# Routed rows of a mixture-of-experts layer: 31 pair tiles and nine single tiles in place of 39 pair tiles

## The chip, the cores and the metric

The kernel runs on one core of one Trainium2 chip. The metric is device time in microseconds (us) of one execution. Before the change the median of three executions is 734.16 us (734.12 to 734.52). What differs by less than about 0.2% (1.5 us) can hardly be told from no change.

## The reference

4096 tokens of 128 numbers pass through a feed-forward block, an attention-like block and the same feed-forward block again. The kernel's two feed-forward layers are the part that matters here:

```
x = x + 0.5 * ffn(layernorm(x))
# ffn(flat), E = 8 experts, TOPK = 2, F = 512, D = 128
probs = softmax(flat @ gate_W.T);  top_v, top_i = top_k(probs, 2)
g = silu(flat @ w1_e[e]);  u = flat @ w3_e[e];  out_e = (g * u) @ w2_e[e]
routed = sum over the two chosen experts of gate * out_e
shared = (silu(flat @ w1_s) * (flat @ w3_s)) @ w2_s / 8
ffn = 0.5 * shared + 0.5 * routed
```

Each token is multiplied with the weights of its two chosen experts only. So 8192 rows (token, expert) are sorted by expert and computed in tiles of 128 rows; each expert's rows are padded to whole units.

## The kernel before, in words

The program is written out by engine (`block.tensor`, `block.vector`, `block.scalar`, `block.gpsimd`, `block.sync`), with semaphores by hand. `pipelined(eng, stages, count, ...)` writes out steps k = 0, 1, 2, ...; in step k each stage works on item k minus its lag, in the order in which the stages are listed.

A feed-forward layer l (0 or 1) has these parts.

* **Norm, scores, shared part.** TensorE transposes the normalised tokens and computes gate scores. The shared weights need no routing, so `in_shared` (six matmuls of 512 columns) and `out_shared` (into `psH`) start before the routing is known and fill TensorE while VectorE, ScalarE and TensorE make the routing tables.
* **Routing.** VectorE picks two experts for each token, TensorE ranks the rows (`rank`), and `slots_of` (L826 to L856) turns ranks into row positions: a chain of small VectorE instructions, each waiting for the one before it (`route.then`). Two `shared_steps(1)` around it hand one shared tile each to TensorE. Then 16 batches: VectorE's `batch` (L866, L869), ScalarE's `pairs` (L1165, L1168) and TensorE's `batch` (L1421, columns 2 x `TILES_R`) invert the permutation; `table` (L889 to L902) gives `source` and `target`, and `experts` gives `w_off`, the expert of each pair.
* **Routed part.** GpSimd fetches the rows of each tile with an indirect DMA (`fetch_row`, L626) and later scatters the results (`send_result`, L641); the fetch of group g (four tiles) stands with the send of group g - 5. TensorE, step by step: `in_routed` (lag 4), `look_up` (lag 5: the register reads of the expert offset), `out_routed` (lag 6), and the transposes of the next group's rows (`transpose_rows`, L1433, four at once in every fourth step). Layer 0 leaves one chunk of the shared part (four shared tiles) for after the routed part, layer 1 two chunks; layer 0 goes on to the attention, layer 1 loads `YF` (both results of each token) and adds them.

A pair is 256 rows of one expert. ScalarE copies the pair's weights in two parts of an fp32 split (`weights_of`, L1229: `w_high`, `w_low`, 128 x 1024 each). In `in_routed` 128 x 128 pieces of these weights are stationary and the 256 rows move, so the hidden values come out with the hidden index on the partitions, as `out_routed` needs them as its stationary side:

```
for j in range(FT // PT):
    f = s.u % PT * (FT // PT) + j
    i = product(out[:, s.u % 2, j * PAIR:(j + 1) * PAIR], w_high[n][:, w, cols],
                w_low[n][:, w, cols], high, low)
```

For each tile that makes twelve matmuls of 256 columns (six for `psG`, six for `psU`); ScalarE applies silu (L1155), VectorE multiplies (`gated_routed`, L954, into `hT`), and `out_routed` (L1487) does four fp32 matmuls, which appear as eight instructions. `copy_y` (L980, the last group: `copy_y_last`, L966) scales four tiles' results by their gates into `yout`.

With 39 pairs there are RUN = 78 tiles in GROUPS = 20 groups, the last with LAST = 2 tiles.

## Time and profile before

| | |
|---|---|
| median of three executions | 734.16 us (734.12 to 734.52) |
| span of the profiled execution | 733.5 us; its own device time is not listed, the three executions lie 0.6 to 1.0 us above this span |
| TensorE matmul busy | 660.3 us, 90% of the span |
| TensorE weight load busy | 602.1 us, 82% |
| VectorE, ScalarE, GpSimd busy | 458.8, 411.3, 430.6 us |
| routed part, layer 0 / layer 1 | 112.4 to 301.8 us / 512.3 to 701.5 us |
| attention | about 316 to 440 us |

Matmuls are pipelined: an instruction's own duration is longer than the distance from its start to the next one's start, so the distance between starts, not the mean duration, tells what a matmul costs in a stream. "Busy" counts the union of overlapping instructions. A row's bracket gives the time that the engine sat idle before it and the instruction that ended the wait.

### The profile page before, as it was taken

To read this page: it belongs to the slowest core of one execution; us is meant where nothing else is said; L and a number is where in the kernel's file an instruction comes from. 1 tells how busy PE (TensorE), PEld (TensorE's weight loads), DVE (VectorE), ACT (ScalarE), POOL (GpSimd) and SP (SyncE) were. 2 spreads that over 40 slices of the span, in tenths; PEclk is the share of its full clock that TensorE was granted. 3 is DMA by queue.
4 is the path that set the end of the run, shared out by engine and by line. 5 is a ranking of instruction groups with operands and counts; after the bars stand their busy time and mean duration, and the time that the engine had idled before them with its cause. 6 is when DMAs were issued, how large, how long until landed. Compare 5 with 4: busy or idle time off the path is not lost.

```text
span 733.5 us, 14294 instructions
## 1 busy us (share of the span) xinstructions
PE 660.3 (90%) x4860; PEld 602.1 (82%) x4860; DVE 458.8 (63%) x1177; ACT 411.3 (56%) x861; POOL 430.6 (59%) x511
## 2 busy tenths in 40 slices
PE   3878999999999999957987777999999999999995
PEld 3767879999999999825654574888999999999983
DVE  6678895554445555359999867884555555544536
ACT  2658617666666666236654436664666666666520
POOL 5600075777777776489987424007577777777530
PEclk9989999999999999989999997999999999999999
DMA  9542011221222231131100002402212212212137
GB/s 296 231 78 40 1 42 38 56 52 52 52 55 52 52 53 44 57 105 44 47 12 1 0 1 46 73 2 49 40 55 54 52 52 56 51 53 52 43 104 261
DMA packets 35685, 45.91 MB, mean 63 GB/s; under 512 B 6432, under 2 KB 27936, under 8 KB 35232
## 3 DMA queue, kind: packets, MB, share of 16 engines
q1 hardware_dynamic: 25632, 24.39, 11.8%
q0 software_dynamic: 9984, 20.63, 11.5%
q8 instruction: 40, 0.66, 0.4%
q14 instruction: 29, 0.24, 0.1%
HBM read 28.41 MB, written 16.58 MB: 61 GB/s over the span
## 4 chain that ended last, share of the span: by engine, by line
PE 65%; DVE 20%; issue 4%; ACT 4%; POOL 3%; DMA 2%; SPq 1%; ACTq 0%; POOLq 0%; DVEq 0%
PE psY L1487 18%; PE psG L1334 6%; PE psU L1336 6%; PE psG L1336 6%; PE psU L1335 6%; PE psG L1335 6%; PE psU L1334 6%; PE psH L1405 4%; DVE rec L1076 3%; PE psT L1433 2%; DVE hs L748 2%; DVE XN L738 2%; DVE ln_stats L725 1%; DVE xn L1060 1%; POOL results L641 1%
## 5 line engine op out<-in xcount | busy, mean ns | idle before, releaser
L626 POOL DMA_INDIRECT rows<-tokens,source x156 | 153.7, 985 | 156.3 <-DVE source L900 98.6
L1155 ACT ACTIVATE silu<-psG 128x512 f32<-128x512 f32 x220 | 131.1, 596 | 150.6 <-PE psG L1336 147.2
L954 DVE TENSOR_TENSOR hT<-silu,psU 128x512 f32<-128x512 f32 x156 | 107.4, 688 | 158.9 <-PE psU L1336 150.3
L641 POOL DMA_INDIRECT results<-yout,target x156 | 153.8, 986 | 63.3 <-issue 45.7
L1487 PE MATMUL psY<-W,hT 128*128 x1232 | 162.4, 275 | 1.8 <-DVE yout L980 1.8
L1487 PEld LDWEIGHTS psY<-W,hT 128*128 128x128 f32 x1232 | 150.4, 191 | 2.2 <-DVE hT L954 2.2
L1229 ACT ACTIVATE w_high<-W13H 128x1024 fp32r x78 | 82.7, 1061 | 59.0 <-PE psU L1336 54.8
L1334 PE MATMUL psG<-xTH,w_high 128*128 128x256 f32 x312 | 100.0, 321 | 0.7 <-ACT w_low L1229 0.7
L1336 PE MATMUL psG<-xTH,w_low 128*128 128x256 f32 x312 | 88.0, 282 | 0.0
L1336 PE MATMUL psU<-xTH,w_low 128*128 128x256 f32 x312 | 88.0, 282 | 0.0
L1335 PE MATMUL psU<-xTL,w_high 128*128 128x256 f32 x312 | 87.7, 281 | 0.0
L1335 PE MATMUL psG<-xTL,w_high 128*128 128x256 f32 x312 | 87.4, 280 | 0.0
L1334 PE MATMUL psU<-xTH,w_high 128*128 128x256 f32 x312 | 86.9, 278 | 0.0
L1229 ACT ACTIVATE w_low<-W13L 128x1024 fp32r x78 | 81.8, 1048 | 0.0
L748 DVE TENSOR_TENSOR hs<-silu,psU 128x512 f32<-128x512 f32 x64 | 43.7, 684 | 38.3 <-PE psU L1336 30.5
L1405 PEld LDWEIGHTS psH<-W2S,hs 128*128 128x128 f32 x512 | 59.4, 192 | 5.7 <-DVE hs L748 4.7
L1405 PE MATMUL psH<-W2S,hs 128*128 128x128 f32 x512 | 60.1, 276 | 2.9 <-DVE hs L748 2.9
L1334 PEld LDWEIGHTS psG<-xTH,w_high 128*128 128x128 f32 x312 | 59.2, 190 | 0.9 <-issue 0.9
L1335 PEld LDWEIGHTS psG<-xTL,w_high 128*128 128x128 f32 x312 | 59.3, 190 | 0.0
L1334 PEld LDWEIGHTS psU<-xTH,w_high 128*128 128x128 f32 x312 | 59.1, 190 | 0.0
L1336 PEld LDWEIGHTS psG<-xTH,w_low 128*128 128x128 f32 x312 | 58.8, 188 | 0.0
L1335 PEld LDWEIGHTS psU<-xTL,w_high 128*128 128x128 f32 x312 | 58.6, 188 | 0.0
(188 smaller groups left out, 1215.7 us busy)
## 6 DMA issues: line engine op xcount, KB each, us to landing
W<-w_e SPq DMA_DIRECT2D x3, 2048.0 KB, 13.7
tokens<-XN SPq DMA_DIRECT2D x16, 260.0 KB, 5.9
Y<-results SPq DMA_DIRECT2D x32, 128.0 KB, 2.2
YF<-results SPq DMA_DIRECT2D x16, 256.0 KB, 5.9
rows<-tokens,source POOLq DMA_INDIRECT x156
results<-yout,target POOLq DMA_INDIRECT x156, 2.3
X<-x SPq DMA_DIRECT2D x8, 256.0 KB, 5.5
out<-X SPq DMA_DIRECT2D x8, 256.0 KB, 2.8
```

What stands on the lines that cost most here:

```text
L626: pool.indirect_dma_start(rows[:, slot(l, g), t, :], None, tokens, bass.IndirectOffsetOnAxis(ap=source[:, tile:tile + 1], axis=0))\
L641: pool.indirect_dma_start(results, bass.IndirectOffsetOnAxis(ap=target[:, tile:tile + 1], axis=0), yout[:, g % 2, t, :], None).then_inc(y_ ...
L748: dve.tensor_tensor(hidden, silu[:, s.u % 2, :], psU[:, s.u % 2, :], ALU.mult).then_inc(h_done, 1)
L954: dve.tensor_tensor(hT[:, s.u // PT % 2, half, :].rearrange("p f c -> p (f c)"), silu[:, s.u % 2, :], psU[:, s.u % 2, :], ALU.mult).then_i ...
L1076: dve.reciprocal(rec[:, s.u, :, :], den[:, s.u, :, :]).then_inc(y_link, 1)
L1155: act.activation(silu[:, s.u % 2, :], psG[:, s.u % 2, :], ACT.Silu).then_inc(silu_done, 1)
L1229: act.activation(used[p % 2][:, :, :], kept[:, :, bass.ds(entries[p], F)], ACT.Copy)\
L1334: pe.matmul(out, a_high, b_high, start=True, stop=False)
L1335: pe.matmul(out, a_high, b_low, start=False, stop=False)
L1336: return pe.matmul(out, a_low, b_high, start=False, stop=True)
L1405: i = pe.matmul(psH[:, par, t * D:(t + 1) * D], hs[:, par, f, t * P:(t + 1) * P], W2S[:, f, :], start=(f == 0), stop=(f == FT - 1))
L1487: i = pe.matmul(into[:, t * D:(t + 1) * D], hT[:, s.u // PT % 2, f, s.u % PT * P:(s.u % PT + 1) * P], W2[:, bass.ds(at + f * D, D)], start ...
```

## The change

There are PAIRS = 31 pairs, followed by SINGLES = 9 single tiles of 128 rows: UNITS = 40, RUN = 71 tiles, 18 groups, the last with three tiles. An expert with n tiles gets n // 2 pairs and, for an odd n, one single (with more than 31 pairs in all, those beyond become singles). A single tile is computed the other way round: its rows (`xTH`, `xTL`, 128 x 128) are stationary and the expert's weights move, 512 columns each, straight out of `W13H` and `W13L`: six matmuls of 512 columns and no copy by ScalarE. The hidden values then come out with the rows on the partitions, so VectorE writes them into `hrow`, TensorE turns them with four transposes into `psH` (`turn_hidden`), ScalarE copies `psH` into `turned` (`copy_turned_h`), and `out_routed` takes `turned`. `slots_of` gets more instructions, and `TILES_R` falls from 78 to 71.

```diff
-PAIRS = TOPK * NT // PAIR + E - 1
-RUN = PT * PAIRS
+PAIRS = 31
+SINGLES = 9
+UNITS = PAIRS + SINGLES
+RUN = PT * PAIRS + SINGLES
...
-        last_y = [psY, psT]
+        last_y = [psY, psT, psH[:, 0, :]]
...
+                    route.then(dve.tensor_tensor_scan(single_at[:, 1:E + 1], ones[:, 0:E], nsingle[:, :], 0.0,
+                                                      ALU.mult, ALU.add))
...
+                    route.then(dve.tensor_tensor(beyond, cum[:, :, :], wide(singles_from[:, :], ET_FLAT), ALU.is_gt))
+                    route.then(dve.tensor_tensor(beyond, beyond, wide(moved_by[:, :], ET_FLAT), ALU.mult))
+                    route.then(dve.tensor_tensor(cum[:, :, :], cum[:, :, :], beyond, ALU.add))
...
+                    if s.i >= PT * PAIRS:
+                        dve.tensor_tensor(hrow[:, s.i % 2, :], silu[:, s.u % 2, :], psU[:, s.u % 2, :], ALU.mult)\
+                           .then_inc(h_done, 1)
+                        return
...
+                def copy_turned_h(i):
+
+                    act.wait_ge(turned_psum, SINGLES * l + i - PT * PAIRS + 1)
+                    act.activation(turned[:, i % 2, :, :].rearrange("p f c -> p (f c)"), psH[:, i % 2, :], ACT.Copy)\
+                       .then_inc(turned_done, 1)
...
+                    if k - 1 >= PT * PAIRS:
+                        copy_turned_h(k - 1)
...
+                    if s.i >= PT * PAIRS:
+                        at = table_entry(l, s)
+                        own_high, own_low = xTH[:, par, s.u % GT, :], xTL[:, par, s.u % GT, :]
+                        for out, w, used, full in ((psG, 0, silu_done, g_full), (psU, 1, h_done, u_full)):
+                            pe.wait_ge(used, turn - 1)
+                            product(out[:, s.u % 2, :], own_high, own_low, W13H[:, w, bass.ds(at, F)],
+                                    W13L[:, w, bass.ds(at, F)]).then_inc(full, 1)
+                        return
...
+                def turn_hidden(s):
+
+                    if s.i < PT * PAIRS:
+                        return
+                    pe.wait_ge(h_done, s.i + first_routed[l] + 1)
+                    for f in range(FT):
+                        i = pe.transpose(psH[:, s.i % 2, f * P:(f + 1) * P], hrow[:, s.i % 2, f * P:(f + 1) * P],
+                                         ident[:, :])
+                    i.then_inc(turned_psum, 1)
...
+                pipelined(pe, [(in_routed, 4), (turn_hidden, 5), (look_up_in, 3), (look_up, 5), (out_routed, 6),
+                               (transpose_later, 0)], RUN, 2 * GT, straight=True)
```

The order of instructions shows the two places on which most rests. First TensorE in the routed part. Before, the second half of a pair's `in_routed` and the `out_routed` behind it (TENSOR_LOAD and ISA are register reads; twelve matmuls of 256 columns make one tile, the first four stand above this piece):

```order
L1335 MATMUL psG<-xTL,w_high 128x256
L1336 MATMUL psG<-xTH,w_low 128x256
L1334 MATMUL psU<-xTH,w_high 128x256
L1335 MATMUL psU<-xTL,w_high 128x256
L1336 MATMUL psU<-xTH,w_low 128x256
L1334 MATMUL psU<-xTH,w_high 128x256
L1335 MATMUL psU<-xTL,w_high 128x256
L1336 MATMUL psU<-xTH,w_low 128x256
L1345 TENSOR_LOAD w_off
L1345 ISA x2
L1494 ISA x2
L1487 MATMUL psY<-W,hT 128x128 x4
```

Of the changed kernel, a step among the single tiles:

```order
L1385 MATMUL psU<-W13H,xTH 128x512
L1386 MATMUL psU<-W13L,xTH 128x512
L1387 MATMUL psU<-W13H,xTL 128x512
L1544 MATMUL psH<-ident,hrow 128x128 x4
L1397 TENSOR_LOAD w_off
L1397 ISA x2
L1575 ISA
L1576 ISA
L1569 ISA
L1562 MATMUL psY<-W,turned 128x128 x4
L1385 MATMUL psG<-W13H,xTH 128x512
```

The `psU` matmuls belong to tile i + 1, the transposes to tile i, and the `psY` matmuls to tile i - 1: the four transposes and one more register read per tile stand between them.

Second VectorE in `slots_of`, between the ranks and the first batch. Before:

```order
L830 TENSOR_SCALAR pair_bits<-psY 128x8
L831 TENSOR_SCALAR pair_bits<-pair_bits 128x8
L833 CAST npair<-pair_bits 128x8
L834 SCALAR_TENSOR_TENSOR tend<-ones,npair 128x8
L836 TENSOR_TENSOR tstart<-tend,npair 128x8
L837 SCALAR_TENSOR_TENSOR base<-tstart,psY 128x8
```

In the changed kernel, from behind `base` on (up to `base` there is one instruction more than before):

```order
L858 TENSOR_TENSOR nsingle<-pair_at 128x8
L860 SCALAR_TENSOR_TENSOR nsingle<-nsingle,ntile 128x8
L862 SCALAR_TENSOR_TENSOR single_at<-ones,nsingle 128x8
L865 TENSOR_SCALAR singles_from<-pair_at 128x8
L866 SCALAR_TENSOR_TENSOR moved_by<-pair_at,single_at 128x8
L868 TENSOR_SCALAR moved_by<-moved_by 128x8
L870 SCALAR_TENSOR_TENSOR chosen<-base,chosen 128x8
L872 SCALAR_TENSOR_TENSOR cum<-not_first,chosen 128x256
L764 TENSOR_TENSOR hs<-silu,psU 128x512
L879 TENSOR_TENSOR pick<-cum,singles_from 128x256
L880 TENSOR_TENSOR pick<-pick,moved_by 128x256
L881 TENSOR_TENSOR cum<-cum,pick 128x256
```

In all, seven small instructions more than before stand ahead of the scan and the shared tile (`hs`), and three of 128 x 256 behind it.

## Rows read from the trace of the kernel before

**Rows 1.** The page, part 1: TensorE's busy time, share of the span and instructions
```profile
PE 660.3 (90%) x4860; PEld 602.1 (82%) x4860; DVE 458.8 (63%) x1177; ACT 411.3 (56%) x861; POOL 430.6 (59%) x511
```

**Rows 2.** Windows: busy time of each engine by stretch, then granted clock, DMA share, GB/s
```profile
55.00:70.00 15.00, 13.08 (x95) 10.98 (x95) 14.15 (x54) 13.20 (x44) 0.00 (x0) 1.00 0.34 49
...
150.00:200.00 50.00, 50.00 (x437) 50.00 (x436) 25.02 (x46) 32.84 (x43) 38.25 (x39) 1.00 0.21 53
...
450.00:470.00 20.00, 18.80 (x96) 14.06 (x95) 19.25 (x66) 10.10 (x37) 0.24 (x1) 0.79 0.64 107
```

**Rows 3.** Timeline of TensorE, routed part: start us, length us, instruction
```profile
119.74 1.05 PE L1487 MATMUL psY<-W,hT 128*128 x8
...
122.05 1.05 PE L1487 MATMUL psY<-W,hT 128*128 x8
122.94 0.60 PE L1433 MATMUL psT<-ident,rows 128*128 128x128 f32 x4
...
124.79 1.05 PE L1487 MATMUL psY<-W,hT 128*128 x8
```

**Rows 4.** Timeline of TensorE, shared part: matmuls of 512 columns
```profile
61.28 0.39 PE L1335 MATMUL psU<-XNTL,W13SH 128*128 128x512 f32 x1
...
61.52 0.39 PE L1336 MATMUL psU<-XNTH,W13SL 128*128 128x512 f32 x1
```

**Rows 5.** Timeline, first matmul of the routed part, layer 0
```profile
112.42 0.36 PE L1334 MATMUL psG<-xTH,w_high 128*128 128x256 f32 x1 [0.70 <-ACT w_low L1229]
```

**Rows 6.** Timeline, all engines, end of the routed part of layer 0
```profile
299.24 0.69 DVE L980 TENSOR_TENSOR yout<-psY,gate 128x512 f32<-128x512 f32 x1
...
300.07 1.13 PE L1487 MATMUL psY<-W,hT 128*128 x8 [0.87 <-DVE yout L980]
...
300.20 0.97 POOL L641 DMA_INDIRECT results<-yout,target  x1 [4.43 <-DVE yout L980]
...
301.85 0.48 PE L1334 MATMUL psG<-XNTH,W13SH 128*128 128x512 f32 x1
...
306.59 0.97 POOL L641 DMA_INDIRECT results<-yout,target  x1 [0.30 <-issue]
```

**Rows 7.** The same for layer 1 and what follows it
```profile
701.50 0.48 PE L1334 MATMUL psG<-XNTH,W13SH 128*128 128x512 f32 x1
...
706.22 0.97 POOL L641 DMA_INDIRECT results<-yout,target  x1 [0.30 <-issue]
...
715.59 0.69 DVE L1001 TENSOR_TENSOR X<-X,YF 128x512 f32<-128x512 f32 x1 [6.13 <-DMA YF<-results]
...
716.93 0.50 PE L1334 MATMUL psU<-XNTH,W13SH 128*128 128x512 f32 x1 [1.28 <-DVE hs L748]
```

**Rows 8.** Timeline, routing of layer 0: slots_of on VectorE, and who waits behind it
```profile
50.90 0.17 DVE L831 TENSOR_SCALAR pair_bits<-pair_bits 128x8 int32<-128x8 int32 x1
...
51.10 0.17 DVE L833 CAST npair<-pair_bits 128x8 f32<-128x8 int32 x1
...
57.63 0.56 ACT L1165 ACTIVATE pair<-in_tile,partition 128x312 bf16<-128x312 bf16 x1 [1.80 <-DVE in_tile L866]
...
62.54 0.43 PE L1421 MATMUL psT<-pair,at_place 128*128 128x156 bf16 x4 [0.64 <-ACT pair L1168]
```

**Rows 9.** The same wait of TensorE in layer 1
```profile
468.50 0.43 PE L1421 MATMUL psT<-pair,at_place 128*128 128x156 bf16 x4 [0.64 <-ACT pair L1168]
```

**Rows 10.** Groups, shapes kept apart: busy us, mean ns of one, idle us before
```profile
L847 DVE TENSOR_TENSOR pick<-cum,onehot 128x256 f32<-128x256 f32 x4 | 2.5, 617 | 0.1
...
L796 DVE TENSOR_TENSOR onehot<-rev_e,row_b 128x256 f32<-128x256 f32 x4 | 1.7, 424 | 0.1
...
L1168 ACT ACTIVATE pair<-in_tile 128x78 bf16<-128x78 bf16 x128 | 23.2, 253 | 0.0
L1165 ACT ACTIVATE pair<-in_tile,partition 128x312 bf16<-128x312 bf16 x32 | 17.5, 548 | 5.5 <-DVE in_tile L866 5.5
...
L1133 ACT ACTIVATE XNT<-psH 128x512 f32<-128x512 f32 x10 | 6.0, 595 | 10.7 <-PE psH L1380 10.5
```

More of the change, by code:

```diff
@@ L275, in macaron @@
         cum = memory["cum"]
-        pair_cmp = memory["pair_cmp"]
+        unit_cmp = memory["unit_cmp"]
         memory = overlaid(
             [("hT", [P, 2, FT, PAIR], fp32),
-             ("yout", [P, 2, GT, D], fp32)],
+             ("yout", [P, 2, GT, D], fp32),
+             ("hrow", [P, 2, F], fp32)],
             [("XN", [P, TILES, ROW], fp32)])
@@ L284, in macaron @@
         yout = memory["yout"]
+        hrow = memory["hrow"]
         XN = memory["XN"]
@@ L325, in macaron @@
              ("w_high1", [P, 2, F], fp32r)],
+            [("below_turned", [P, 6 * 2 * F], fp32),
+             ("turned", [P, 2, FT, P], fp32)],
             [("XNTL", [P, NT], fp32r), ("XNTH", [P, NT], fp32r)])
@@ L344, in macaron @@
         w_low = [memory[f"w_low{n}"] for n in range(2)]
+        turned = memory["turned"]
         psG = ps("psG", [P, 2, 512])
@@ L405, in macaron @@
         y_psum = sem("y_psum")
+        turned_psum = sem("turned_psum")
+        turned_done = sem("turned_done")
         y_done = sem("y_done")
@@ L829, in slots_of @@
                     dve.wait_ge(ranked, l + 1)
-                    route.then(dve.tensor_scalar(pair_bits[:, 0, :], psY[:, E:2 * E], float(PAIR - 1), None, ALU.add))
-                    route.then(dve.tensor_scalar(pair_bits[:, 1, :], pair_bits[:, 0, :], PAIR.bit_length() - 1, None,
+                    route.then(dve.tensor_scalar(tile_bits[:, 0, :], psY[:, E:2 * E], float(P - 1), None, ALU.add))
+                    dve.tensor_scalar(tile_bits[:, 1, :], tile_bits[:, 0, :], P.bit_length() - 1, None,
+                                      ALU.logical_shift_right)
@@ L835, in slots_of @@
                                                       ALU.mult, ALU.add))
-                    route.then(dve.tensor_tensor(tstart[:, :], tend[:, :], npair[:, :], ALU.subtract))
-                    dve.scalar_tensor_tensor(base[:, :], tstart[:, :], float(PAIR), psY[:, 0:E], ALU.mult, ALU.add)\
+                    route.then(dve.tensor_scalar(pair_at[:, 1:E + 1], pair_sum[:, :], float(PAIRS), None, ALU.min))
+                    dve.scalar_tensor_tensor(base[:, :], pair_at[:, 0:E], float(PAIR), psY[:, 0:E], ALU.mult, ALU.add)\
@@ L873, in experts @@
                 def experts():
[L875 to L879 removed]
+                    for first, n, at in ((0, PAIRS, pair_at), (PAIRS, SINGLES, single_at)):
+                        cmp3 = [P, n, E]
+                        i = dve.tensor_tensor(unit_cmp[:, first:first + n, :], wide(unit_no[:, 0:n], cmp3),
+                                              at[:, 1:E + 1].unsqueeze(1).to_broadcast(cmp3), ALU.is_ge)
+                    route.then(i)
+                    route.then(dve.tensor_reduce(unit_e[:, :], unit_cmp[:, :, :], X_AXIS, ALU.add))
+                    dve.tensor_scalar(w_off[:, :], unit_e[:, :], float(E - 1), float(F),
                                       ALU.min, ALU.mult).then_inc(w_off_done, 1)
@@ L1484, in out_routed @@
                     t = s.u % GT
-                    into = last_y[t % 2] if s.i >= RUN - LAST else psY
+                    into = last_y[t] if s.i >= RUN - LAST else psY
                     for f in range(FT):
-                        i = pe.matmul(into[:, t * D:(t + 1) * D], hT[:, s.u // PT % 2, f, s.u % PT * P:(s.u % PT + 1) * P],
+                        hidden = turned[:, s.i % 2, f, :] if single else \
+                            hT[:, s.u // PT % 2, f, s.u % PT * P:(s.u % PT + 1) * P]
+                        i = pe.matmul(into[:, t * D:(t + 1) * D], hidden,
                                       W2[:, bass.ds(at + f * D, D)], start=(f == 0), stop=(f == FT - 1))
@@ L1491, in look_up, with look_up_in @@
                 def look_up(s):
-                    if s.u % PT == 0:
+                    if s.u % PT == 0 or s.i >= PT * PAIRS:
                         for f in range(FT):
                             pe.lower_ap(W2[:, bass.ds(table_entry(l, s) + f * D, D)])
-                pipelined(pe, [(in_routed, 4), (look_up, 5), (out_routed, 6), (transpose_later, 0)], RUN, 2 * GT,
-                          straight=True)
+                def look_up_in(s):
+                    if s.i >= PT * PAIRS:
+                        at = table_entry(l, s)
+                        for w in range(2):
+                            pe.lower_ap(W13H[:, w, bass.ds(at, F)])
+                            pe.lower_ap(W13L[:, w, bass.ds(at, F)])
+                pipelined(pe, [(in_routed, 4), (turn_hidden, 5), (look_up_in, 3), (look_up, 5), (out_routed, 6),
+                               (transpose_later, 0)], RUN, 2 * GT, straight=True)
                 def sum_results(n):
```

59 lines of the change are left out of this document (38 added, 21 removed).

## The prediction

 Each of the two routed parts takes 189 us: layer 0 from 112.42 [rows 5] to 301.85, where the first shared matmul behind it starts [rows 6]. Together they are half of the span. There a tile less is a tile's TensorE time less, and a TensorE instruction more is paid in full. In the routing stretches it is otherwise: between 55 and 70 us VectorE is busy 14.15 of 15 us, between 450 and 470 us 19.25 of 20 [rows 2], and TensorE waits 0.64 us at a time for ScalarE's `pair`, which itself waited for VectorE's `in_tile` [rows 8, 9].
>
> **Prices on TensorE.** The starts count, not the durations. From one `psY` block to the next are 122.05 - 119.74 = 2.31 us: one tile's `in_routed` and `out_routed`. The eight `psY` instructions take 122.94 - 122.05 = 0.89 us of it, so twelve matmuls of 256 columns take 1.42 us, 0.118 each. With the four row transposes a step takes 124.79 - 122.05 = 2.74 us, so four transposes cost 0.43 to 0.44 us, 0.11 each [rows 3]. A matmul of 512 columns costs 61.52 - 61.28 = 0.23 to 0.24 us [rows 4]; six of them are 1.38 us over the stretch that I read. Check: 78 x 2.31 + 19 x 0.44 + the wait of 0.87 us [rows 6] = 189.4 us, as measured.
>
> **What each routed part loses.** Seven tiles less (78 to 71): 7 x 2.31 = 16.2 us, and their row transposes, 7 x 0.11 = 0.8 us. The wait of 0.87 us for `yout` at the end [rows 6] goes as well: it arises because the first tile of the last group comes right behind the last tile of the group before, with no `in_routed` between; with a last group of three tiles an `in_routed` and four transposes lie there (1.82 us), more than VectorE's 0.69 us. Sum 17.8 us.
>
> **What it gains.** Nine singles: 9 x 0.44 = 4.0 us for turning the hidden values. Their `in_routed` costs 6 x 0.23 = 1.38 against 1.42 us, 9 x 0.04 = 0.4 us less. ScalarE's new copy of 128 x 512 costs 0.60 us like the copy of the same form [rows 10], while two weight copies per pair fall away; I cost it at nothing on TensorE, because between the transposes of tile i and `out_routed` of tile i lie `out_routed` of tile i - 1 (0.89) and the next step's `in_routed` and transposes (1.82): 2.7 us of cover for some 0.8 us. Likewise between the end of `in_routed` i and its transposes lie 0.44 + 0.89 + 1.38 = 2.7 us, for VectorE's 0.69 us. Without that cover it would cost what the rivals say. Only for the very last tile, with no `in_routed` behind it, do I add 0.1 us. Sum 3.7 us; TensorE's routed part gets 14.1 us shorter.
>
> **Where it reaches the result.** What follows the routed part waits for GpSimd's last send, which starts 306.59 - 301.85 = 4.74 us after TensorE is through: six sends of 1.28 us, (306.59 - 300.20) / 5 apart, queued behind the last full group [rows 6]. Now there are seven, but TensorE still has 1.38 + 2 x 0.44 + 3 x 0.89 + 0.1 = 5.0 us to go after the last full group; it had 301.85 - 299.2 = 2.65. So the last send starts at 1.0 (yout and start) + 6 x 1.28 - 5.0 = 3.7 us after TensorE's end, 1.1 us sooner. In layer 0 that is 14.1 + 1.1 = 15.2 us. In layer 1, VectorE stands 6.13 us waiting for `YF`, and TensorE at 716.93 waits 1.28 us for VectorE in turn [rows 7]; the loads decide, and TensorE's lag of 1.1 us is within its slack: 15.2 us again. Together 30.4 us.
>
> **GpSimd** issues 142 DMAs a layer in place of 156: 14 x 1.28 = 17.9 us less, more than TensorE loses, so it is no nearer to being the bound. The removed weight copies on ScalarE (16 in a layer) were hidden and bring nothing.
>
> **What the routing costs.** `slots_of` has seven more small instructions at 51.10 - 50.90 = 0.20 us each [rows 8], 1.4 us, and three of 128 x 256. The nearest forms take 0.42 (L796) and 0.62 us (L847) [rows 10], with 0.04 us between two; they read and write in order like the first, so I take 0.46 each, 1.4 us; the upper bound is 2.0. VectorE is the bound there and hands over to ScalarE and by it to TensorE [rows 2, 8, 9], so 2.8 us arrive. Back come: ScalarE's smaller `pair` copies, (548 - 253) / (312 - 78) = 1.26 ns an element [rows 10], 56 elements a batch, 0.07 us for each of some six batches that are bound by it, 0.4 us; and 64 `psT` matmuls of 142 in place of 156 columns, at 0.23 us for 512 [rows 4] 0.4 us. Net 2.0 us a layer, 4.0 in all. It has bounds of 0 (slack of VectorE takes it up before TensorE notices) and 3.4 a layer (nothing given back).
>
> **Sum.** 30.4 - 4.0 = 26.4 us off the span of 733.5 us: 707.1. The three executions lie 0.6 to 1.0 above that span; from their median of 734.16 I forecast **707.8 us**. The unknown terms alone (routing 0 to 6.8, the cover of the last tile, 0.23 or 0.24 for a matmul) give 704 to 711.
>
> **A rule that speaks against it.** The row shows four transposes in 0.60 us, starting 0.11 apart, so the fourth alone lasts 0.27 [rows 3]. The Trainium skill's page "TensorE: Matmul & The Clock Gate", section "Part 4: PE-mode transpose", gives about 275 ns for a transpose of 128 x 128 in one kernel, and most of it as access latency. Read as a cost of each, it would make 72 transposes dearer by 0.165 us each, 11.9 us, and the sum 719.7; the duration agrees with the trace, the spacing says that it overlaps. The same section says that transposes do not count as busy for the clock. Both are rivals below, worked out from rows.
>
> **Rivals.**
> * **Routing hidden.** VectorE's 2.8 us are taken up by its waits. For it: it waits 1 to 2 us in some places of the shared part. Against it: TensorE is nearly full behind 70 us and can't catch up what it has lost. 707.8 - 4.0 = 703.8.
> * **A handoff shows.** Three engines in turn (VectorE's `hrow`, TensorE, ScalarE's `turned`) per single where there was one. If the copy and its start, 0.6 + 0.2 us, stand in TensorE's way in each of 18 tiles, 14.4 us: 722.2; in part, or by the register reads now made for every single, 712 to 716. Against it: the cover of 2.7 us above.
> * **Transposes don't overlap.** 4 x 0.27 = 1.08 in place of 0.44 us, 18 times: 11.5 us, 719.3. Against it: [rows 3].
> * **Serial singles, slower than before.** The place is the step of a single: if one `psH` or `hrow` half or the order made each tile wait for the whole chain of the same tile, it would take 1.38 + 0.85 (product and start) + 0.60 (transposes to their end) + 0.8 + 0.89 = 4.5 us in place of 2.7: 18 x 1.8 = 32.4 us, 740.2. It turns the sign from 1.46 us a tile on (26.4 / 18). For it: nothing in the order, which puts tile i + 1 and i - 1 around tile i.
> * **Clock, slower than before.** If the stretch of singles, with 0.44 of 2.7 us in transposes, were granted 1.2 GHz, 18 x 2.7 = 48.8 us come on top: 756.6. Against it: the routed part is granted 1.00 with a group of transposes in every fourth step [rows 2, 3].
> * **Nothing gained.** Another queue sets the end and the time stays near 734. No row speaks for it.
>
> **How the numbers follow.** Forecast 0.62; routing hidden 0.15; a handoff shows 0.14; transposes don't overlap 0.03; serial 0.03; clock 0.02; nothing 0.01. Faster by more than 0.2% (1.5 us, about what can be told from no change): 0.62 + 0.15 + 0.14 + 0.03 = 0.94; within 0.01; slower 0.05. The range of 703 to 718 takes in the forecast's own 704 to 711, the hidden routing and the lower half of the handoffs; it leaves out 0.07 + 0.03 + 0.03 + 0.02 + 0.01 = 0.16.
>
> **What would show it.** Right: among the singles, `psY` blocks about 2.7 us apart and no idle time before `psH` or `psY`; the first routed matmul about 2 us later in layer 0 and 2 us more in its distance from the routing of layer 1; TensorE's routed part 175 us long; the last send 3.7 us behind it. Wrong: idle time before `psY` released by ScalarE's `turned` or before `psH` released by VectorE's `hrow`; transposes 0.27 us apart; a granted clock under 1.00 at the end of the routed part; or a routed part that starts as early as before, which would move the time towards 703.8.

## The result and the profile after

The changed kernel took 712.42 us (median of four executions, 711.56 to 713.63) against 734.34 us (734.12 to 735.35, four executions) of the kernel before on the same chip: a ratio of 0.9701, 95% interval 0.9688 to 0.9714. It is 21.9 us faster, where 26.4 were forecast. The sign was right and the time lies in the stated range of 703 to 718; it is 4.6 us above the forecast's 707.8, and also above the 704 to 711 that the prediction's own unknown terms gave. One execution of the second experiment below took 1337.39 us and is outside its ratio.

The page of the changed kernel, part 1, answers to [rows 1]:

```profile
PE 637.3 (90%) x4530; PEld 573.0 (81%) x4530; DVE 443.3 (62%) x1167; ACT 382.3 (54%) x833; POOL 402.0 (57%) x485
```

TensorE has 330 matmuls and 23.0 us of busy time less, and is still busy for 90% of the span. What bounds the kernel is the same engine as before. Windows at the same places of the program as in [rows 2] (the third starts 9.4 us behind the `row_a` of layer 1, as there):

```profile
55.00:70.00 15.00, 11.93 (x79) 9.39 (x79) 14.06 (x50) 11.25 (x34) 0.00 (x0) 1.00 0.29 48
...
150.00:200.00 50.00, 50.00 (x433) 50.00 (x432) 24.68 (x45) 31.89 (x41) 38.11 (x40) 1.00 0.21 54
...
438.41:458.41 20.00, 18.66 (x86) 13.96 (x84) 19.00 (x69) 7.81 (x28) 0.23 (x1) 0.70 0.60 109
```

In the routing (first window) TensorE does less in the same time, 79 instructions in place of 95, since VectorE, busy for 14.06 of 15 us, hands over later. In the third window the granted clock is 0.70, where it was 0.79. That isn't what moves the routing: in the experiment with both operands at 32 the same stretch has

```profile
436.92:456.92 20.00, 15.31 (x86) 11.05 (x84) 19.00 (x69) 7.70 (x28) 0.21 (x1) 0.93 0.57 109
```

with VectorE busy for the same 19.00 us, and from `row_a` to the first routed matmul it takes 73.71 us, against 73.84. In the routed part TensorE is full as before, but the second window has 433 instructions in place of 437. That small row turns out to be most of the error.

**The singles.** Timeline of TensorE in layer 0, where the singles begin (start us, length us, instruction):

```profile
268.09 0.60 PE L1544 MATMUL psH<-ident,hrow 128*128 128x128 f32 x4
268.53 1.06 PE L1562 MATMUL psY<-W,hT 128*128 x8
270.83 0.60 PE L1544 MATMUL psH<-ident,hrow 128*128 128x128 f32 x4
271.27 1.06 PE L1562 MATMUL psY<-W,turned 128*128 x8
272.16 0.49 PE L1485 MATMUL psT<-ident,rows 128*128 128x128 f32 x3
273.89 0.60 PE L1544 MATMUL psH<-ident,hrow 128*128 128x128 f32 x4
```

From `psH` to `psH` are 270.83 - 268.09 = 2.74 us, the forecast's "about 2.7"; four transposes delay the `psY` block behind them by 271.27 - 270.83 = 0.44 us, and no row shows idle time before `psH` or `psY`. The chain VectorE, TensorE, ScalarE is covered. A single's own turn, all engines:

```profile
276.62 0.60 PE L1544 MATMUL psH<-ident,hrow 128*128 128x128 f32 x4
276.89 0.69 DVE L992 TENSOR_TENSOR hrow<-silu,psU 128x512 f32<-128x512 f32 x1 [0.78 <-PE psU L1387]
...
277.26 0.60 ACT L1283 ACTIVATE turned<-psH 128x512 f32<-128x512 f32 x1 [0.54 <-PE psH L1544]
...
279.79 1.06 PE L1562 MATMUL psY<-W,turned 128*128 x8
```

`turned` is ready at 277.86 and needed at 279.79, where the `psY` block of that tile starts: 1.9 us to spare. ScalarE waits 0.54 us for the transposes; nobody waits for that wait. The groups say the same for all 18 singles:

```profile
L1283 ACT ACTIVATE turned<-psH 128x512 f32<-128x512 f32 x18 | 10.7, 597 | 10.1 <-PE psH L1544 10.1
...
L1544 PE MATMUL psH<-ident,hrow 128*128 128x128 f32 x72 | 10.8, 272 | 0.0
```

The 10.1 us of idle time are ScalarE's, which is busy for 54% of the span; TensorE's idle time before `psH` is 0.0.

**Start and end of the routed parts**, which answer to [rows 5, 6, 7]:

```profile
114.55 0.36 PE L1385 MATMUL psG<-xTH,w_high 128*128 128x256 f32 x1 [0.72 <-ACT w_low L1271]
...
287.32 0.96 POOL L657 DMA_INDIRECT results<-yout,target  x1 [6.14 <-DVE yout L1022]
...
288.88 0.60 PE L1544 MATMUL psH<-ident,hrow 128*128 128x128 f32 x4
...
290.21 1.12 PE L1562 MATMUL psH<-W,turned 128*128 x8
...
291.08 0.47 PE L1385 MATMUL psG<-XNTH,W13SH 128*128 128x512 f32 x1
...
294.96 0.97 POOL L657 DMA_INDIRECT results<-yout,target  x1 [0.30 <-issue]
...
679.20 0.47 PE L1385 MATMUL psG<-XNTH,W13SH 128*128 128x512 f32 x1
...
683.09 0.97 POOL L657 DMA_INDIRECT results<-yout,target  x1 [0.30 <-issue]
```

The routed part of layer 0 is 291.08 - 114.55 = 176.53 us long (189.43 before), the last `psY` block (its output is `psH` there) has no wait for `yout` before it, and the last send starts 3.88 us behind TensorE's end (4.74 before).

**Where the 23.7 us went**, from the starts of the same instructions in both traces:

| stretch | before | after | difference | forecast |
|---|---|---|---|---|
| start to first routed matmul, layer 0 | 112.42 | 114.55 | +2.13 | +2.0 |
| routed part, layer 0 | 189.43 | 176.53 | -12.90 | -14.1 |
| to the last send | 4.74 | 3.88 | -0.86 | -1.1 |
| last send to `row_a` of layer 1 | 134.00 | 134.04 | +0.04 | 0 |
| `row_a` to the first fetch of layer 1 | 53.65 | 55.56 | +1.91 | +2.0 |
| first fetch to first routed matmul | 18.06 | 18.28 | +0.22 | 0 |
| routed part, layer 1 | 189.20 | 176.36 | -12.84 | -14.1 |
| to the last send | 4.72 | 3.89 | -0.83 | -1.1 |
| last send to the end | 27.28 | 26.71 | -0.57 | 0 |
| span | 733.5 | 709.8 | -23.7 | -26.4 |

The first and the last row hold a part that isn't the change's. The same program profiled again has its first routed matmul at 113.70, 0.85 us sooner, and ends 27.49 us behind the last send, 0.78 us later; all rows between repeat to 0.04 us. Where the 0.85 us come from shows at VectorE's first `row_a`, ahead of everything that the change touches (the kernel before, the changed kernel, and the changed kernel again):

```profile
36.10 0.41 DVE L800 TENSOR_REDUCE row_a<-logit 128x32 f32<-128x256 f32 x1
```

```profile
36.30 0.41 DVE L816 TENSOR_REDUCE row_a<-logit 128x32 f32<-128x256 f32 x1
```

```profile
35.49 0.41 DVE L816 TENSOR_REDUCE row_a<-logit 128x32 f32<-128x256 f32 x1
```

From there to the first routed matmul are 76.32, 78.25 and 78.21 us: the routing of layer 0 costs 1.93 and 1.89 us, beside 1.91 in layer 1. So the routing's two terms came as forecast. The misfit is in the routed parts: 1.2 and 1.3 us each.

**What failed there.** The price of a pair's step. Both traces, `psY` blocks in layer 0: the second and the 48th behind it, with twelve groups of row transposes between. In the kernel before, the first block is the one at 119.74 of [rows 3]:

```profile
235.74 1.05 PE L1487 MATMUL psY<-W,hT 128*128 x8
```

And in the changed kernel:

```profile
121.86 1.05 PE L1562 MATMUL psY<-W,hT 128*128 x8
...
238.90 1.05 PE L1562 MATMUL psY<-W,hT 128*128 x8
```

48 steps took 235.74 - 119.74 = 116.00 us before and 238.90 - 121.86 = 117.04 us after: 0.022 us more for each, without idle time, at a granted clock of 1.00 in both. The same instructions in the same order, 0.9% slower. What could do that? The diff changes no line of `in_routed` for pairs. But tables with 71 in place of 78 columns are smaller, and the tiles allocated behind them move. The start addresses that the allocator gives (`xTH` 137632, now 137664; `w_high` 212160, now 211552; `XNTH` at the same places as `w_high`) put `w_high` and `XNTH` at 32 modulo 64 bytes, where they were at 0, and `xTH` at 0, where it was at 32. The experiments begin there.

### The profile page after: what moved, and what is told of

Its sections match the earlier page's. It is cut to its first block, busy times and chain, and to the rows that moved or that the text cites. A ratio compares the mean times of both kernels' runs of the same rounds, so it can differ in the third digit from the quotient of the medians.

```text
span 709.8 us, 13472 instructions
## 1 busy us (share of the span) xinstructions
PE 637.3 (90%) x4530; PEld 573.0 (81%) x4530; DVE 443.3 (62%) x1167; ACT 382.3 (54%) x833; POOL 402.0 (57%) x485
## 4 chain that ended last, share of the span: by engine, by line
PE 65%; DVE 21%; ACT 4%; issue 4%; POOL 2%; DMA 2%; SPq 1%; POOLq 0%; ACTq 0%; DVEq 0%
PE psY L1562 17%; PE psG L1385 6%; PE psU L1385 6%; PE psU L1387 6%; PE psU L1386 6%; PE psG L1387 6%; PE psG L1386 6%; PE psH L1457 5%; DVE rec L1118 3%; PE psT L1485 2%; DVE hs L764 2%; DVE XN L754 2%; DVE ln_stats L741 1%; DVE xn L1102 1%; PE psH L1544 1%
## 5 line engine op out<-in xcount | busy, mean ns | idle before, releaser
L996 DVE TENSOR_TENSOR hT<-silu,psU 128x512 f32<-128x512 f32 x124 | 85.2, 687 | 125.7 <-PE psU L1387 119.0
L1562 PE MATMUL psY<-W,hT 128*128 x992 | 130.8, 275 | 0.0
L1562 PEld LDWEIGHTS psY<-W,hT 128*128 128x128 f32 x992 | 121.1, 191 | 0.3
L1271 ACT ACTIVATE w_high<-W13H 128x1024 fp32r x62 | 65.7, 1060 | 47.3 <-PE psU L1387 42.6
L1385 PE MATMUL psG<-xTH,w_high 128*128 128x256 f32 x248 | 79.9, 322 | 0.7 <-ACT w_low L1271 0.7
L1386 PE MATMUL psU<-xTL,w_high 128*128 128x256 f32 x248 | 70.0, 282 | 0.0
L1386 PE MATMUL psG<-xTL,w_high 128*128 128x256 f32 x248 | 69.9, 282 | 0.0
L1387 PE MATMUL psG<-xTH,w_low 128*128 128x256 f32 x248 | 69.7, 281 | 0.0
L1387 PE MATMUL psU<-xTH,w_low 128*128 128x256 f32 x248 | 69.7, 281 | 0.0
L1387 PEld LDWEIGHTS psU<-xTH,w_low 128*128 128x128 f32 x248 | 47.0, 189 | 0.0
```

The costliest lines, as they stand in the source:

```text
L996: dve.tensor_tensor(hT[:, s.u // PT % 2, half, :].rearrange("p f c -> p (f c)"), silu[:, s.u % 2, :], psU[:, s.u % 2, :], ALU.mult).then_i ...
L1271: act.activation(used[p % 2][:, :, :], kept[:, :, bass.ds(entries[p], F)], ACT.Copy)\
L1385: pe.matmul(out, a_high, b_high, start=True, stop=False)
L1386: pe.matmul(out, a_high, b_low, start=False, stop=False)
L1387: return pe.matmul(out, a_low, b_high, start=False, stop=True)
L1562: i = pe.matmul(into[:, t * D:(t + 1) * D], hidden, W2[:, bass.ds(at + f * D, D)], start=(f == 0), stop=(f == FT - 1))
```

## Experiments

Theory A: the missing 2.7 us are the price of the new start addresses. Rival: the edit itself makes the stream of matmuls slower, by the register reads for each single or by ScalarE's and VectorE's added work. "Kernel before" stands for its runs on the same chip as the experiment: 735.18 us for the first four, then 734.78, 735.38 and 734.85. "48 steps" is the distance measured above.

### 32 bytes ahead of `pair`

```
              ("in_tile", [P, DEEP, BATCH, TILES_R], bf16),
+             ("pad", [P, 8], fp32),
              ("pair", [P, DEEP, BATCH, 2, TILES_R], bf16),
```

> The changed kernel with 32 bytes of unused memory per partition ahead of `pair`, so that `silu`, `XNTH`, `XNTL`, `w_high`, `w_low` and `turned` start again at a multiple of 64 bytes, as in the kernel before. Theory A (the smaller tables shifted these tiles by 608 bytes, to 32 beyond a multiple of 64, and matmuls that read them got slower): six shared matmuls back from 1.40 to 1.37 us, a pair step from 2.33 to 2.31 us, and the time 706.5 to 709.5 us. Theory B (the slower matmuls belong to that execution or chip, not to the addresses): the time stays at 711.5 to 713.5 us, the steps at 1.40 and 2.33.

708.92 us (707.41 to 709.89), ratio 0.9642 (0.9629 to 0.9655); span 705.7, 27.8 under before's. Its `psY` blocks:

```profile
121.24 1.05 PE L1563 MATMUL psY<-W,hT 128*128 x8
...
237.16 1.05 PE L1563 MATMUL psY<-W,hT 128*128 x8
```

48 steps take 115.92 us; a routed part takes 289.09 - 113.92 = 175.17 us, the forecast's 175; shared steps take 1.37 us as before (1.40 in the changed kernel). The time is 3.5 us under the changed kernel's by the medians, 4.3 by the ratios, and the span 4.1 us. Of the span, 1.36 and 1.48 us are the two routed parts. Another 1.26 us are the stretch from the last send of layer 0 to `row_a` of layer 1, 132.78 us in place of 134.04; that goes with the granted clock, not with the pair steps (see the shorter routing chain below). With before's pace the routed parts come out as the prediction summed them. Theory A stood here.

### The same pad in the kernel before

```
+             ("pad", [P, 8], fp32),
```

> The kernel before with the same 32 bytes inserted, so that these tiles start 32 bytes beyond a multiple of 64. Theory A: shared matmuls 1.40 us, pair steps 2.33 us or more, time 737 to 740 us. Theory B: as before, 734.3 within 1 us.

733.57 us, ratio 0.9974 (0.9963 to 0.9984): 0.3% faster, not slower. A miss of theory A as I had put it. The shared steps did go to 1.40 us, but the pairs went the other way:

```profile
118.60 1.05 PE L1488 MATMUL psY<-W,hT 128*128 x8
...
233.32 1.05 PE L1488 MATMUL psY<-W,hT 128*128 x8
```

114.72 us for 48 steps, less than any other kernel here. So addresses change the pace of a kernel in which nothing else changes, but "w at 32 is bad" is not the rule. TensorE waits 3.2 us for `yout` in this kernel (1.8 in the kernel before), which takes part of the gain back.

### A longer routing chain in the kernel before

```
+                    for n in range(7):
+                        route.then(dve.tensor_tensor(tstart[:, :], tend[:, :], npair[:, :], ALU.subtract))
...
+                    for n in range(3):
+                        route.then(dve.tensor_tensor(pick[:, :, :], onehot[0][:, :, :], onehot[1][:, :, :], ALU.mult))
```

> The kernel before with seven more small chained VectorE instructions ahead of the shared tile in `slots_of` and three more of 128 x 256 behind it (their results are not used). My theory: 2.8 us of VectorE arrive at the first routed matmul of each layer as 2.0 to 2.8 us, since nothing is given back here by smaller tables: time 738.3 to 740. Rival (VectorE's waits take it up): the first routed matmul as before, time 734.3 within 1 us.

741.16 us (735.18 before), ratio 1.0084 (1.0070 to 1.0099), above the expected 738.3 to 740; span 739.1, which is 5.6 us more: 2 x 2.8, the forecast's price of the chain without anything given back. The first routed matmul of layer 0:

```profile
114.72 0.36 PE L1338 MATMUL psG<-xTH,w_high 128*128 128x256 f32 x1 [0.72 <-ACT w_low L1233]
```

That is 2.30 us later than in [rows 5], but this execution was 0.48 us ahead at `row_a` already:

```profile
35.62 0.41 DVE L800 TENSOR_REDUCE row_a<-logit 128x32 f32<-128x256 f32 x1
```

From `row_a` to the first routed matmul are 79.10 us, 2.78 more than before, and `row_a` to the first fetch of layer 1 is 499.46 - 443.04 = 56.42, 2.77 more. VectorE's chain arrives on TensorE whole. The rival "routing hidden" is out. The changed kernel has +1.93 and +1.91 over the same stretches, so 0.85 and 0.86 us a layer come back there; 0.8 had been forecast for its smaller tables. (That the smaller tables are what gives it back was not tested by itself.) 48 steps take 116.00 us, to the hundredth what the kernel before has: the pace is no matter of chance from run to run.

### 27 pairs and 17 singles

```
-PAIRS = 31
-SINGLES = 9
+PAIRS = 27
+SINGLES = 17
```

> The changed kernel with 27 pairs and 17 singles, again 71 tiles: 16 tiles of the two layers go from half a pair to a single. My theory: a single step is 2.73 us, a half pair 2.33, so 16 x 0.40 = 6.4 us more than the changed kernel: 718 to 720 us, with no waits in front of the transposes or of psY. Rival (handoffs begin to show in a longer row of singles): over 722 us, with idle time before psH or psY.

716.94 us (715.52 to 717.82), ratio 0.9747 (0.9734 to 0.9761), against 0.9701; the expected 718 to 720 was missed from below, the rival's 722 more widely. The routed part of layer 0:

```profile
114.73 0.36 PE L1385 MATMUL psG<-xTH,w_high 128*128 128x256 f32 x1 [0.69 <-ACT w_low L1271]
...
293.58 0.48 PE L1385 MATMUL psG<-XNTH,W13SH 128*128 128x512 f32 x1
```

178.85 us, 2.32 more than the 176.53 of the changed kernel. Its own addresses differ too (48 steps 116.32 us, so 54 pair steps are 54 x 0.015 = 0.8 us quicker), which makes 8 singles dearer than 8 pair tiles by 3.1 us, 0.39 each; the prediction's price was 0.44 - 0.04 = 0.40. The expectation had left the placing out: it gives back some 0.8 us a layer here, and the stretch up to `row_a` of layer 1 is 132.39 us, 1.65 under the changed kernel's. No row shows idle time before `psH` or `psY`, so the handoffs cost nothing with 17 singles in a row either. More singles than are needed to avoid padding is a loss.

### The placing of before by offsets modulo 64 alone

To the pad of the first experiment comes one ahead of `xTH`, so that `xTH` (32) and `w_high` (0) have the offsets of before:

```
-            [("xTH", [P, 2, GT, P], fp32r), ("xTL", [P, 2, GT, P], fp32r)],
+            [("pad_x", [P, 8], fp32), ("xTH", [P, 2, GT, P], fp32r), ("xTL", [P, 2, GT, P], fp32r)],
```

> The changed kernel with one more 32-byte pad than the first experiment, ahead of xTH: now xTH starts at 32 and w, silu and XNTH at 0 (offsets modulo 64 bytes), which is the placing of the kernel before in full. Theory A (the offsets of the two operands set the step's pace, and nothing else of the placing matters): pair steps without transposes 2.306 us, steps of the shared part 1.37 us, both as in the first experiment, and its time within 0.5 us, 708.4 to 709.4 us. Rival (what helped was that xTH and w stood at the same offset): steps of 2.32 us, and 710 to 711.5 us.

711.61 us (709.63 to 713.46), ratio 0.9689 (0.9670 to 0.9709). Its `psY` blocks:

```profile
121.36 1.05 PE L1563 MATMUL psY<-W,hT 128*128 x8
...
238.40 1.05 PE L1563 MATMUL psY<-W,hT 128*128 x8
```

48 steps take 117.04 us, the pace of the changed kernel, so theory A in this form fell: the operands' offsets modulo 64 don't set the pair step. The shared steps are at 1.37 us, as expected.

This run is worth more than the theory that it was made for. `pad_x` stands in memory that is lent and given back, so against the first experiment two tiles alone move, `xTH` and `xTL`, by 32 bytes each, and the 48 steps go from 115.92 to 117.04 us. The start of these operands by itself changes the pace.

### Both operands at 32

`pad_x` as above, and 32 bytes between `XNTL` and `XNTH`:

```
-            [("XNTL", [P, NT], fp32r), ("XNTH", [P, NT], fp32r)])
+            [("XNTL", [P, NT], fp32r), ("pad_n", [P, 8], fp32), ("XNTH", [P, NT], fp32r)])
```

> The changed kernel with pads so that xTH and w both start at 32 modulo 64 bytes, while XNTH starts at 0. Theory A (each operand's offset sets the pace): pair steps of 2.273 us as in the second experiment and shared steps of 1.37 us, 124 x 0.033 = 4.1 us under the first experiment, 705 us (704 to 706.5). Rival (in the second experiment the pair steps were fast for another reason, such as the absolute place in a larger power of two): pair steps of 2.30 us and no gain over 708.9 us. A third case: TensorE's gain is taken back by waits for yout, and the time falls by under 2 us.

709.61 us (709.03 to 710.63), ratio 0.9657 (0.9640 to 0.9675). 48 steps take 116.32 us: a miss again (705 was expected), near the rival's 2.30 us per step. Shared steps are 1.39 us. Against the changed kernel `xTH` and `xTL` moved by 32 bytes and `XNTH`, which these steps don't read: 116.32 in place of 117.04 us, the other way round from the move before.

### A shorter routing chain

On top of the kernel before this one: `nsingle` goes, the sum of all tiles leaves VectorE's chain, and five small operations move to GpSimd.

```
+                pool.tensor_scalar(twice[:, :], pair_at[:, 1:E + 1], -float(PT), None, ALU.mult)\
...
+                pool.tensor_tensor(single_at[:, 1:E + 1], twice[:, :], tile_sum[:, :], ALU.add).then_inc(move_link, 1)
...
+                pool.tensor_tensor(moved_by[:, :], twice[:, :], single_at[:, 0:E], ALU.add).then_inc(move_link, 1)
...
-                    route.then(dve.tensor_tensor(nsingle[:, :], pair_at[:, 1:E + 1], pair_at[:, 0:E], ALU.subtract))
...
```

> As the experiment with both operands at 32, and the chain of small operations that the change added to VectorE's routing is shortened: one is dropped, one scan is taken out of the chain, and four or five go to GpSimd, beside VectorE's own chain; what is computed stays. If the chain stands on the path as forecast (2.0 us a layer for seven small and three larger ones), the first routed matmul of layer 0 comes some 0.9 us sooner and the time falls by 1.5 to 2 us under that experiment: 703 to 704 us. If the slots' DMAs or the exchange wait are later for it on GpSimd, no change or up to 1 us slower.

708.49 us (706.36 to 709.68), ratio 0.9637 (0.9616 to 0.9658), 1.1 us under the kernel without it, where 1.5 to 2 were expected (and 703 to 704 us in all, counted from the 705 that the kernel without it had missed). The intervals overlap, so the times alone would not settle it; the trace does. The first routed matmul of that kernel, and of this one:

```profile
113.87 0.36 PE L1385 MATMUL psG<-xTH,w_high 128*128 128x256 f32 x1 [0.69 <-ACT w_low L1271]
```

```profile
112.98 0.36 PE L1396 MATMUL psG<-xTH,w_high 128*128 128x256 f32 x1 [0.70 <-ACT w_low L1282]
```

0.89 us sooner, as expected (0.84 counted from `row_a`), and `row_a` to first fetch in layer 1 is 54.70 against 55.50. Of these 1.7 us the span shows 1.2. About 1.0 us is lost between the last send of layer 0 and `row_a` of layer 1 (135.14 against 134.12 us). There the granted clock (the third number from the end) differs, without this kernel and with it:

```profile
365.00:385.00 20.00, 14.64 (x58) 9.73 (x56) 19.62 (x74) 10.54 (x48) 15.43 (x27) 0.91 0.00 1
```

```profile
365.00:385.00 20.00, 16.10 (x57) 11.31 (x58) 19.59 (x78) 9.61 (x45) 14.06 (x25) 0.83 0.00 1
```

The fourteen traces of this document agree on it, each read some 72 to 92 us behind the last send of layer 0, where this window lies. With a granted clock of 1.00 there (the first experiment, offsets as before, and 27 pairs with 17 singles) the stretch takes 132.16 to 132.78 us; with 0.91 (ten traces) 133.86 to 134.33; with 0.83 (this kernel) 135.14. No experiment set the clock, so which of the two follows from the other is not shown; but up to 3 us of a span can lie in this stretch, whatever was changed elsewhere.

### The changed kernel once more

> The changed kernel itself once more, beside the same runs of the kernel before as the three experiments of this call, so that the effect of the pads can be read on one chip: 712.4 us by its earlier ratio, with pair steps of 2.325 us and shared steps of 1.40 us.

712.00 us (711.35 to 712.44), ratio 0.9690 (0.9673 to 0.9706); span 709.8 and 48 steps of 117.04 us, both as the first time (start and end of the span differ by 0.85 and 0.78 us, as said above, and cancel). It ran beside the same executions of the kernel before as the last three experiments, so what differs between those four is the programs' own.

### All tiles placed as in the second experiment, or as in the kernel before

Four pads, ahead of `xTH`, `hT`, `pair` and `silu`, give all tiles of the routed part the addresses of another kernel modulo 128 bytes, and in full from `pair` on. Of the second experiment:

```
+            [("pad_x", [P, 24], fp32), ("xTH", [P, 2, GT, P], fp32r), ("xTL", [P, 2, GT, P], fp32r)],
+        pad_h = sb("pad_h", [P, 16])
+             ("pad_p", [P, 32], fp32),
+             ("pad_s", [P, 112], fp32),
```

> The changed kernel with pads that give xTH, xTL, hT, yout, XNT, hs, silu, the gathered rows and all weight tiles the start addresses of the second experiment, modulo 128 bytes (xTH 32, hT 0, w 96), those from pair on in full. The fifth and sixth experiment have shown that the offsets of xTH and w modulo 64 bytes don't settle the pace alone. Theory B (the placing of all these tiles modulo 128 bytes sets it, whatever the rest of the program is): pair steps of 2.273 us as there, 124 x 0.052 = 6.4 us of TensorE's time under the changed kernel, of which waits for yout may take some back: 706 to 709 us. Rival (the pace hangs on something else in the program, such as where its instructions come to lie in time against those of the other engines): steps of 2.30 to 2.325 us and 709 to 712 us.

709.97 us (709.20 to 710.69), ratio 0.9662 (0.9647 to 0.9677); 48 steps 115.92 us, not 114.72.

Of the kernel before (`pad_p` of 24 in place of 32 numbers):

> The changed kernel with pads that give the same tiles the start addresses of the kernel before modulo 128 bytes (xTH 32, hT 0, w 64), those from pair on in full. Theory B: pair steps of 2.306 us and shared steps of 1.37 us as there, and 709 us. Rival: 2.325 us and 1.40 us, 711 to 712 us.

711.98 us (711.33 to 714.27), ratio 0.9692 (0.9674 to 0.9711); 48 steps 117.03 us, not 116.00. Theory B, residues modulo 128, fell in both.

### The kernel before, placed as the changed kernel

```
+            [("pad_x", [P, 8], fp32), ("xTH", [P, 2, GT, P], fp32r), ("xTL", [P, 2, GT, P], fp32r)],
+        pad_h = sb("pad_h", [P, 16])
+             ("pad_p", [P, 8], fp32),
+             ("pad_s", [P, 16], fp32),
```

> The kernel before with pads that give the same tiles the start addresses of the changed kernel modulo 128 bytes (xTH 64, hT 64, w 96). Theory B: pair steps of 2.325 us in place of 2.307, shared steps of 1.40 us in place of 1.37, 156 x 0.018 + 32 x 0.03 = 3.8 us slower than the kernel before. Rival: no change within 1 us.

738.10 us (737.32 to 738.52), ratio 1.0041 (1.0026 to 1.0055), span 736.5: 2.7 us slower by the medians and 3.0 in span, where 3.8 were expected, without a single instruction changed. Here `xTH` and `hT` have the changed kernel's addresses in full, and `w_high` its address plus 768.

```profile
119.51 1.05 PE L1490 MATMUL psY<-W,hT 128*128 x8
...
236.55 1.05 PE L1490 MATMUL psY<-W,hT 128*128 x8
```

48 steps take 117.04 us, the changed kernel's figure to the hundredth, and a shared step 1.40 us. Its routed parts are 191.01 and 190.86 us long in place of 189.43 and 189.20. This is the counterpart of the first experiment: the old program with the new placing is slow, the new program with another placing is fast. The rival, that the edit slows the stream of pairs, is out.

### Distance of 64, with the shorter routing

The distances from `xTH` up to `w_high`, modulo 256, ordered the kernels so far. The last run took the distance that the second experiment had, 64:

```
+             ("pad_p", [P, 40], fp32),
-            [("XNTL", [P, NT], fp32r), ("pad_n", [P, 8], fp32), ("XNTH", [P, NT], fp32r)])
+            [("XNTL", [P, NT], fp32r), ("pad_n", [P, 32], fp32), ("XNTH", [P, NT], fp32r)])
```

with `pad_x` taken out of the kernel with the shorter routing.

> The changed kernel with the shortened routing of the seventh experiment, and pads that put w 64 bytes above xTH modulo 256, and XNTH at 0 modulo 64. Theory C, formed on the placings so far: the pair step's pace goes by the distance from xTH's start up to w's, modulo 256 bytes. Distance 160 gave 2.325 to 2.332 us in five kernels, 192 gave 2.306 and 2.307, 128 gave 2.310 and 2.314, 32 gave 2.301 to 2.315, and 64 gave 2.273 in the only kernel that had it, the second experiment. So here 2.273 us, and the shared steps, which went by XNTH's start modulo 64 in all kernels, at 1.37 us: 124 x 0.041 = 5.1 us of TensorE's time in the pairs and 32 x 0.02 = 0.6 us in the shared steps under the seventh experiment's 708.5 us, so 703 us (702 to 706, since TensorE may wait for yout as it did there). Rival (that 64 was fast by chance of something else): steps of 2.30 us or more and 707.5 to 709 us.

706.28 us (705.01 to 706.88), ratio 0.9607 (0.9594 to 0.9620), span 705.2: the lowest median of all, 28.6 us under the kernel before and 6.1 under the changed kernel by their medians; the shorter routing has its share in that.

```profile
120.56 1.06 PE L1574 MATMUL psY<-W,hT 128*128 x8
...
236.09 1.05 PE L1574 MATMUL psY<-W,hT 128*128 x8
```

48 steps take 115.53 us: faster than every kernel but the second experiment, but not its 114.72. Theory C fell as a rule for the number; the median, 706.28, lies just above its range of 702 to 706 and below the rival's 707.5.

### All placings together

Addresses are modulo 256; the last two columns are `XNTH` modulo 64 and the mean step of the shared part behind the routed part of layer 0 (six matmuls of 512 columns).

| kernel | `xTH` | `w_high` | distance | 48 steps, us | `XNTH` | shared step, us |
|---|---|---|---|---|---|---|
| before; before with longer chain | 160 | 192 | 32 | 116.00 | 0 | 1.37 |
| 27 pairs and 17 singles | 0 | 32 | 32 | 116.32 | 32 | 1.40 |
| before with pad | 160 | 224 | 64 | 114.72 | 32 | 1.40 |
| last experiment | 0 | 64 | 64 | 115.53 | 0 | 1.38 |
| both at 32 | 224 | 96 | 128 | 116.32 | 0 | 1.39 |
| shorter routing | 32 | 160 | 128 | 116.15 | 0 | 1.39 |
| the changed kernel, twice | 192 | 96 | 160 | 117.04 | 32 | 1.40 |
| offsets as before | 224 | 128 | 160 | 117.04 | 0 | 1.37 |
| placed as before | 32 | 192 | 160 | 117.03 | 0 | 1.37 |
| before placed as after | 192 | 96 | 160 | 117.04 | 32 | 1.40 |
| first experiment | 192 | 128 | 192 | 115.92 | 0 | 1.37 |
| placed as the second | 32 | 224 | 192 | 115.92 | 32 | 1.41 |

What the table bears: the four kernels at distance 160 (three pairs of addresses) had the same slow pace, in the old program and in the new, and the two at 192 the same faster one; at 32, 64 and 128 the distance alone doesn't settle it. Between two pairs of rows `xTH` and `xTL` are all that moved among the tiles that the steps read: from the first experiment to "offsets as before" (115.92 to 117.04) and from the changed kernel to "both at 32" (117.04 to 116.32). `XNTH` at 32 modulo 64 always made the shared steps 1.40 us or more, at 0 it made them 1.37 to 1.39. Why this is so stays open, and so does a rule that would give the pace of a new placing. No run tells whether TensorE's own reads are slower at some addresses, or their meeting with reads and writes of the other engines. Moving `w_high` alone, or `xTH` alone through a full set of addresses, was not tried.

## Why the prediction was right, and where it was off

* **Seven tiles less and the wait for `yout` gone** (17.8 us a layer): right in kind. The step that failed is the 2.31 us of a pair's step, carried over from the kernel before to the 62 pair tiles that stay: it took the price of a step as fixed. In the changed kernel a step costs 0.022 us more, in 62 steps 1.3 us a layer, and that is the misfit of the routed parts (176.53 and 176.36 for 175.3). The first experiment, with 115.92 us for 48 steps, has 175.17.
* **Nine singles at 0.40 us**: right, 0.39 by the experiment with 17. The blocks are 2.74 us apart, and the cover of 2.7 us was there: `turned` is ready 1.9 us before it is needed. The tail costs something: from the last `psH` transposes to the last `psY` block are 290.21 - 288.88 = 1.33 us, 0.89 of it the block between, so 0.44 for the transposes themselves and nothing more; the 0.1 us added for the last tile did not appear.
* **Last send 3.7 us behind TensorE's end**: 3.88 and 3.89.
* **Routing 2.0 us a layer**: 1.93 and 1.91, counted from `row_a`. The experiments with a longer chain (+2.78 and +2.77) and a shorter one (-0.84 and -0.80) show that it is on the path in full, and 0.85 us a layer come back where 0.8 were summed.
* **Shared part unchanged**: not quite, 1.40 us a step in place of 1.37, from `XNTH`'s new place. There are 32 such steps a layer (the expectation of the kernel placed as the changed one counted half of them); most stand in the shadow of VectorE during the routing, and their share is small: from `row_a` to the first routed matmul of layer 0 the first experiment, with 1.37 us a step, takes 78.21 us, as the changed kernel does with 1.40 (78.25 and 78.21).
* **From span to time**: the prediction set 0.6 to 1.0 us around the span. In all nine listed executions of the changed kernel it is 1.72 to 1.83 us (711.56 for a span of 709.8). By that, the span of 733.5 belongs to an execution of about 735.2, slower than the median that stood beside it. The forecast span of 707.1 would have become 708.9; this is 1.1 of the 4.6 us. Span for span the forecast was off by 2.7, and the last 0.9 us are the median's distance from the profiled execution, which was the fastest of the four.
* **What was luck.** Not the sign and not the mechanism. But 712.42 us is also what the rival "a handoff shows, in part" gave (712 to 716). The time alone can't tell it from the forecast; the traces do, with no idle time in the routed parts and blocks 2.74 us apart, register reads included.
* **The rivals.** Transposes that don't overlap: four of them take the stream 0.44 us, though each lasts 272 ns. The Trainium skill's figure of about 275 ns ("TensorE: Matmul & The Clock Gate", "Part 4: PE-mode transpose") gives the duration that this trace shows, though it stands beside a figure for bf16 and these are fp32. In the stream here the next one starts 0.11 us later, so the sum by the spacing was the right one. Clock: granted 1.00 throughout the routed parts, singles included (the forecast's 18 x 2.7 for it is 48.6, not 48.8). Serial singles, visible handoffs: no idle time before `psY` or `psH`. Routing hidden: out by the longer chain.

## What to carry to other kernels

Where one engine is full, a price for each step taken from starts, not durations, forecast the removal of steps within a tenth here (12.9 us for 14.1), and work on other engines that lies between two steps of lag was indeed free. But an edit that changes the size of any table also moves every tile behind it, and a stream of matmuls may then run 1% slower or faster with not one instruction changed, as it did here. Take distances from a place that the edit doesn't touch: a stretch counted from the start of the span moved by 0.85 us from one execution of the same program to the next. Compare start addresses before and after, and try a few pads of 32 bytes before a difference of half a per cent is put down to the edit.

## What I had not expected of the hardware

In these kernels the pace of a stream of fp32 matmuls depends on where its operands start in SBUF; moving `xTH` and `xTL` alone by 32 bytes took 48 steps from 115.92 to 117.04 us. Over the thirteen kernels of the table, 48 identical steps (576 matmuls of 256 columns, 48 blocks of `psY` and 48 row transposes) took from 114.72 to 117.04 us, 2.0%, at the full clock with no idle time shown. Each program has its own figure, and it came out the same to 0.01 us when a program ran again (117.04 twice) and when its chain elsewhere was longer (116.00 twice). The difference shows in the twelve matmuls on `xTH` and `w`: by the distances between starts, 0.98 of the 1.04 us between the kernel before and the changed kernel, and the `psY` blocks and transposes keep their time. It is worth 3.2 us in the two routed parts of the kernel before and 2.8 us in those of the changed kernel.
